# Output projection of two heads with three products: the high parts stacked by transfers, the low halves summed on VectorE

## The chip, the cores and the metric

One core of a Trainium2 chip runs the whole program. Its engines (TensorE or PE with its weight loads PEld, VectorE or DVE, ScalarE or ACT, GpSimd or POOL, and the queue SP that issues transfers) run at the same time, each through its own program in order; they meet only at semaphores. The metric is the device time of one launch in microseconds (us); lower is better.

## The reference

Four blocks on x of 4 x 512 x 256 in fp32: attention with low-rank keys and values, a gated feed-forward net, a state-space scan, the feed-forward net again. The change is in the attention's last step.

```python
kv_up = (kv_c @ wkv_up.T).reshape(bs, seq_len, NH, D_NOPE + D_V)   # kv_c: 64 numbers a token
v = kv_up[..., D_NOPE:]
scores = jnp.where(causal, einsum('bqhd,bkhd->bhqk', q, k) * scale, -inf)
probs = softmax(scores)
out = einsum('bhqk,bkhd->bqhd', probs, v).reshape(bs, seq_len, NH * D_V)
return out @ wo.T                                                  # 16 heads -> 256
```

## The kernel before

**Precision by pairs.** TensorE multiplies in a reduced type (fp32r), so each factor is kept as a high part (rounded by ScalarE) and a low part (VectorE subtracts the high part from the exact value), and a product is three matmuls: high·high, high·low, low·high.

**The value side.** The 64 numbers `kv_c` of a token stand for keys and values of all heads. `v_hl` holds their high part in columns 0 to 63 and their low part in 64 to 127, and the per-head map from 64 numbers to the 256 outputs (`wo_a`, `wo_b`) is made once in eight preparation tasks `t_vo` (lines 381 to 400), two heads each. So `values` leaves in `bank[6]`, for four heads of 128 queries (512 columns), the product with the values' high half in partitions 0 to 63 and the one with their low half in 64 to 127. The attention output is the sum of the two.

**The output projection.** `wo_a` holds the high part of the map in both halves of the partitions, `wo_b` its low part in 0 to 63 and its high part in 64 to 127. `out_high` (ScalarE, L881 and L883) copies all 128 partitions of bank 6 to `o_a` and partitions 0 to 63 once more to `o_b`; `out_low` (VectorE, L1211) puts the remainder of partitions 0 to 63 into partitions 64 to 127 of `o_b`. `project` (TensorE) then makes two products of 128 x 256 for each head, `o_a`·`wo_a` (L1600) and `o_b`·`wo_b` (L1602), eight for a unit.

**Units and slots.** A unit is four heads of one tile of 128 queries; a batch has 16 units (`n`), the program 64. With tile i (0 to 3) a unit has i + 1 blocks of keys. Every engine runs slots `s`: TensorE, ScalarE and VectorE each do in slot s a fixed list of steps of several units at once, written out by hand in `pe_slot`, `act_slot` and `dve_slot`. Unit n has its scores in slots n+2 and n+3, its values in slot n+5 and its projection near the end of slot n+6 of TensorE. VectorE ends its slot n+4 with `out_low(n)`; behind it stand, in the next slot, `recip` (L1188), `pt_low` (L1205) and `row_max` (L1153). TensorE waits for `out_low(n)` at the first `values` matmul of unit n+1, since bank 6 exists once; behind that wait stand transposes (L1573) and scores (L649 to L651) that ScalarE and VectorE work on next. `exp` is L846, `normalise` L866, `pt_high` L875.

**The rest.** SP issues the loads at the start, then waits and loads `ssm_nat` for the third block, then stores the output. GpSimd looks up the feed-forward weights until about 540 us.

Of the kernel before, what the change touches and what calls it, by code (L numbers as in the profile page):

```python
# [4 lines left out]
F32 = mybir.dt.float32  # L5
F32R = mybir.dt.float32r
BF16 = mybir.dt.bfloat16
I32 = mybir.dt.int32
ALU = mybir.AluOpType
ACT = mybir.ActivationFunctionType  # L10

P = 128
# [95 lines left out]
def build(nc, x_in, wq_down, wq_up, wq_rope, q_norm_w, wkv_down, kv_norm_w, wkv_up, wk_rope, wo,  # L108
# [3 lines left out]
    with ctx:  # L112
# [58 lines left out]
        wo_b = r1("wo_b", [P, HEADS, DIM], F32R)  # L171
# [31 lines left out]
        o_b = r2("o_b", [P, 2, G, P], F32R)  # L203
# [29 lines left out]
        def sem(name):  # L233
            return ctx.enter_context(nc.semaphore(name))
# [29 lines left out]
        o_hi_s, o_lo_s, y_mm = sem("o_hi_s"), sem("o_lo_s"), sem("y_mm")  # L264
        x_add, f_add, s_add = sem("x_add"), sem("f_add"), sem("s_add")
# [117 lines left out]
        def t_vo(k):  # L383
# [8 lines left out]
            def act(e, o):  # L392
                nc.scalar.copy(wo_a[:, 2 * k:2 * k + 2, :], o[:, :].rearrange("p (h n) -> p h n", h=2))
                return nc.scalar.copy(wo_b[KR:P, 2 * k:2 * k + 2, :], o[KR:P, :].rearrange("p (h n) -> p h n", h=2))

            def dve(e, o):
                return nc.vector.tensor_tensor(wo_b[0:KR, 2 * k:2 * k + 2, :],
                                               o[0:KR, :].rearrange("p (h n) -> p h n", h=2),
                                               wo_a[0:KR, 2 * k:2 * k + 2, :], ALU.subtract)
# [301 lines left out]
        def _(sp_):  # L701
# [30 lines left out]
            sp_.wait_ge(tok, token_count(BATCH, 0))  # L732
            sp_.wait_ge(at_mm, 1 + 3 * BATCH)
            sp_.dma_start(ssm_nat[:, 0, :, :], w_in.rearrange("(c p) d -> p c d", p=P)).then_inc(ssm_in, 16)
            sp_.dma_start(ssm_nat[:, 2, :, :], w_out.rearrange("(c p) d -> p c d", p=P)).then_inc(ssm_in, 16)
            hpc = P // (DIM // 32)
            for c in range(CK):
                sp_.dma_start(ssm_nat[:, 1, c, :],
                              w_dt[c * hpc:(c + 1) * hpc, :].unsqueeze(1).to_broadcast([hpc, DIM // 32, DIM]))\
                    .then_inc(ssm_in, 16)  # L740
# [52 lines left out]
        def _(act):  # L793
# [84 lines left out]
            def out_high(b, n):  # L878
                act.wait_ge(pv_mm, b * BLOCKS + blocks_before(n + 1))
                free_after(act, y_mm, b * UNITS + n - 1)  # L880
                nc.scalar.copy(o_a[:, n % 2, :, :].rearrange("p h d -> p (h d)"), bank[6][:, :])\  # L881
                    .then_inc(o_hi_s, 1)
                nc.scalar.copy(o_b[0:KR, n % 2, :, :].rearrange("p h d -> p (h d)"), bank[6][0:KR, :])\  # L883
                    .then_inc(o_hi_s, 1)
# [204 lines left out]
        def _(dve):  # L1089
# [119 lines left out]
            def out_low(b, n):  # L1209
                dve.wait_ge(o_hi_s, 2 * (b * UNITS + n) + 2)  # L1210
                nc.vector.tensor_tensor(o_b[KR:P, n % 2, :, :].rearrange("p h d -> p (h d)"), bank[6][0:KR, :],  # L1211
                                        o_a[0:KR, n % 2, :, :].rearrange("p h d -> p (h d)"), ALU.subtract)\
                    .then_inc(o_lo_s, 1)
# [289 lines left out]
        def _(pe):  # L1503
# [89 lines left out]
            def project(b, n):  # L1593
                g = n % (HEADS // G)
                pe.wait_ge(o_hi_s, 2 * (b * UNITS + n) + 2)
# [3 lines left out]
                for h in range(G):  # L1599
                    nc.tensor.matmul(bank[7][:, 0:DIM], o_a[:, n % 2, h, :], wo_a[:, g * G + h, :],  # L1600
                                     start=g == 0 and h == 0, stop=False)
                    last = nc.tensor.matmul(bank[7][:, 0:DIM], o_b[:, n % 2, h, :], wo_b[:, g * G + h, :],  # L1602
                                            start=False, stop=g == HEADS // G - 1 and h == G - 1)
# [253 lines left out]
```

## Time and profile before

| | us |
|---|---|
| median of 3 runs | 822.56 (821.38 to 823.37) |
| the profiled execution | 816.43, of it 814.6 in the span |
| first projection to last (L1600) | 85.7 to 561.2 |
| busy in the span: PE, DVE, ACT | 752.5, 675.2, 607.2 |

Busy time of an engine is the time in which at least one of its instructions runs. Durations of neighbours on one engine overlap in the records, so what an instruction costs a full engine is the distance from its start to the next one's start, not its duration. A wait is given as "engine, what it ran next, <- who ended the wait"; "issue" means that the profile shows no one who did.

### The profile page before, as it was taken

Reading aid. Unit: us, or ns where it says so; the run is one execution under the profiler, and the core shown is the slowest. Engines: PE = TensorE matmul, PEld = TensorE weight load, DVE = VectorE, ACT = ScalarE, POOL = GpSimd, SP = SyncE. Lnnn points to the kernel's source line nnn. Section 1 sums busy time; section 2 is a strip of 40 time slices with the busy share of each in tenths; the row PEclk is TensorE's granted clock in tenths of the full one; section 3 lists DMA queues with packets and bytes.
Section 4 is the critical chain, followed back from the end, with each engine's and each line's share of the span. In section 5 each row is a group of like instructions: output and inputs, shape, how many; then the busy total and the mean of one; then the engine's idle time right before and its main releaser. Section 6 shows DMA issues by size and latency. Waiting matters only on the chain.

```text
span 814.6 us, 15156 instructions
## 1 busy us (share of the span) xinstructions
PE 752.5 (92%) x4556; PEld 648.2 (80%) x4556; DVE 675.2 (83%) x2208; ACT 607.2 (75%) x1508; POOL 462.1 (57%) x388
## 2 busy tenths in 40 slices
PE   4788999999999999999998999999998999999998
PEld 4667888888878788888887888777887788897887
DVE  4986899998899998899998899997775878777643
ACT  2457999987999887999987899895436566674222
POOL 0379999999999999999999999910000000000000
PEclk9988999999999999999999999999999999999999
DMA  9710000000000000000000100000000000000000
GB/s 233 241 53 1 2 1 2 1 1 1 1 2 1 1 2 2 1 2 1 2 1 1 40 2 1 1 1 1 1 1 0 1 1 1 1 1 27 27 27 27
DMA packets 15377, 14.54 MB, mean 18 GB/s; under 512 B 5792, under 2 KB 14432, under 8 KB 15040
## 3 DMA queue, kind: packets, MB, share of 16 engines
q1 hardware_dynamic: 13792, 11.41, 4.8%
q0 software_dynamic: 624, 2.12, 0.8%
q8 instruction: 38, 0.62, 0.3%
q14 instruction: 43, 0.35, 0.1%
q10 hardware_dynamic: 880, 0.04, 0.1%
HBM read 11.46 MB, written 2.10 MB: 17 GB/s over the span
## 4 chain that ended last, share of the span: by engine, by line
PE 57%; DVE 16%; ACT 15%; issue 11%; DMA 1%; DVEq 0%; ACTq 0%; SPq 0%
PE bank L649 11%; PE bank L651 11%; PE bank L650 11%; PE bank L1573 6%; ACT prob L866 5%; ACT prob L846 3%; PE bank L1587 2%; PE bank L1590 2%; DVE pt_lo L1205 2%; ACT pt_hi L875 2%; PE bank L1600 2%; PE bank L1602 2%; PE bank L614 1%; DVE o_b L1211 1%; DVE bias_m L1153 1%
## 5 line engine op out<-in xcount | busy, mean ns | idle before, releaser
L782 POOL TENSOR_SCALAR hot<-raw_gu,lut 128x352 f32<-128x352 int32 x120 | 178.1, 1484 | 12.2
L788 POOL TENSOR_TENSOR total<-total,hot 128x352 f32<-128x352 f32 (+1 forms) x168 | 159.4, 949 | 14.0
L846 ACT ACTIVATE prob<-bank,bias_m 128x128 f32<-128x128 f32 (+3 forms) x256 | 136.2, 532 | 19.4 <-DVE bias_m L1153 19.0
L1153 DVE CUSTOM_DVE_ANT_0 bank<-bank,mask 128x128 f32<-128x128 f32 (+3 forms) x256 | 125.8, 495 | 23.5 <-issue 21.9
L866 ACT ACTIVATE prob<-prob,rden 128x128 f32<-128x128 f32 (+3 forms) x224 | 110.6, 545 | 8.2 <-DVE rden L1188 7.3
L1205 DVE TENSOR_TENSOR pt_lo<-bank,pt_hi 128x512 fp32r<-128x512 f32 x160 | 109.1, 682 | 8.7 <-ACT pt_hi L875 8.3
L1573 PE MATMUL bank<-ident,prob 128*128 128x128 f32 x640 | 99.8, 279 | 15.0 <-ACT prob L866 9.1
L875 ACT CAST pt_hi<-bank 128x512 fp32r<-128x512 f32 x160 | 94.1, 589 | 13.0 <-PE bank L1590 7.2
L1573 PEld LDWEIGHTS bank<-ident,prob 128*128 128x128 f32 x640 | 73.3, 141 | 33.4 <-ACT prob L866 18.6
L649 PE MATMUL bank<-kt_hi,qt_hi 128*128 128x128 f32 (+3 forms) x256 | 87.6, 342 | 3.2 <-ACT prob L846 2.5
L782 POOL TENSOR_SCALAR hot<-raw_dn,lut 128x352 f32<-128x352 int32 (+1 forms) x60 | 87.0, 1451 | 6.1
L651 PE MATMUL bank<-kt_hi,qt_lo 128*128 128x128 f32 (+3 forms) x256 | 83.2, 325 | 0.0
L650 PE MATMUL bank<-kt_lo,qt_hi 128*128 128x128 f32 (+3 forms) x256 | 83.2, 325 | 0.0
L1587 PE MATMUL bank<-pt_hi,v_hl 128*128 128x512 f32 x160 | 68.5, 428 | 3.7 <-issue 3.5
L649 PE MATMUL bank<-xt_hi,gu_hi 128*128 128x512 f32 (+1 forms) x176 | 70.2, 399 | 1.7 <-DVE h_f L1345 1.6
L651 PE MATMUL bank<-xt_hi,gu_lo 128*128 128x512 f32 (+1 forms) x176 | 69.5, 395 | 0.0
L650 PE MATMUL bank<-xt_lo,gu_hi 128*128 128x512 f32 (+1 forms) x176 | 69.4, 394 | 0.0
L1600 PE MATMUL bank<-wo_a,o_a 128*128 128x256 f32 x256 | 67.9, 298 | 0.1
L957 ACT ACTIVATE silu<-bank 128x512 f32<-128x512 f32 x40 | 24.0, 600 | 57.5 <-PE bank L651 57.5
L1590 PE MATMUL bank<-pt_lo,v_hl 128*128 128x512 f32 x160 | 63.6, 398 | 0.3 <-DVE pt_lo L1205 0.2
L1602 PE MATMUL bank<-wo_b,o_b 128*128 128x256 f32 x256 | 63.7, 282 | 0.0
L649 PEld LDWEIGHTS bank<-kt_hi,qt_hi 128*128 128x128 f32 x256 | 49.2, 192 | 13.1 <-ACT prob L846 3.6
(215 smaller groups left out, 2092.7 us busy)
## 6 DMA issues: line engine op xcount, KB each, us to landing
x<-in_L_attn_a_x_dram SPq DMA_DIRECT2D x4, 512.0 KB, 8.1
wo_nat<-in_L_attn_a_wo_dram SPq DMA_DIRECT2D x1, 2048.0 KB, 15.5
out_dram<-x SPq DMA_DIRECT2D x16, 128.0 KB, 1.8
wqu<-in_L_attn_a_wq_up_dram SPq DMA_DIRECT2D x2, 768.0 KB, 8.3
wqr<-in_L_attn_a_wq_rope_dram SPq DMA_DIRECT2D x4, 192.0 KB, 7.0
raw_dn<-in_L_ffn_down_idx_dram POOLq DMA_DIRECT2D x1, 688.0 KB, 6.7
raw_gu<-in_L_ffn_gate_idx_dram POOLq DMA_DIRECT2D x1, 640.0 KB, 5.2
raw_gu<-in_L_ffn_up_idx_dram POOLq DMA_DIRECT2D x1, 640.0 KB, 5.7
```

What stands on the lines that cost most here:

```text
L649: nc.tensor.matmul(o, l_hi, r_hi, start=start and k == 0, stop=False)
L650: nc.tensor.matmul(o, l_hi, r_lo, start=False, stop=False)
L651: last = nc.tensor.matmul(o, l_lo, r_hi, start=False, stop=stop and k == n - 1)
L782: nc.gpsimd.tensor_scalar((hot if v else total)[:, 0:n], raw[:, c:c + n], float(v), lut[:, v:v + 1], ALU.is_equal, ALU.mult).then_inc(lut_ ...
L788: nc.gpsimd.tensor_tensor(dst, total[:, 0:n], hot[:, 0:n], ALU.add).then_inc(lut_sum, 1)
L846: nc.scalar.activation(prob[:, n % 2, h, 0:w], bank[2 + h % 2][:, 0:w], ACT.Exp, bias=bias_m[:, n % 2, h:h + 1], scale=-1.0, accum_out=den ...
L866: nc.scalar.activation(prob[:, n % 2, h, 0:w], prob[:, n % 2, h, 0:w], ACT.Copy, scale=rden[:, n % 2, h:h + 1]).then_inc(norm_a, 1)
L875: nc.scalar.copy(pt_hi[:, c % 2, :, :].rearrange("p h d -> p (h d)"), bank[4 + c % 2][:, :])\
L1153: nc.vector.tensor_tensor_reduce(out=bank[2 + h % 2][:, 0:w], in0=bank[2 + h % 2][:, 0:w], in1=mask[:, TB * P - w:TB * P], scale=1.0, scal ...
L1205: nc.vector.tensor_tensor(pt_lo[:, c % 2, :, :].rearrange("p h d -> p (h d)"), bank[4 + c % 2][:, :], pt_hi[:, c % 2, :, :].rearrange("p h ...
L1573: last = nc.tensor.transpose(bank[4 + c % 2][:, h * P:(h + 1) * P], prob[:, n % 2, h, j * P:(j + 1) * P], ident[:, :])
L1587: nc.tensor.matmul(bank[6][:, :], v, pt_hi[:, c % 2, :, :].rearrange("p h d -> p (h d)"), start=j == 0, stop=False)
```

## The change

For two heads there are three products instead of four. VectorE adds the product with the values' low half (partitions 64 to 127 of bank 6) to the remainder, so `o_a` now holds the high part of partitions 0 to 63 above and "remainder plus low half" below, and is multiplied with `wo_a` for each head. `o_b` holds only high parts: that of an even head in partitions 0 to 63, that of the odd head beside it in 64 to 127, multiplied with a `wo_b` that has the map's low parts of the two heads stacked in the same way. Two transfers between SBUF and SBUF for each unit, issued by SP, copy the high parts into `o_b`. The loads of `ssm_nat` come behind the transfers of the first unit of the last batch.

```diff
-        wo_b = r1("wo_b", [P, HEADS, DIM], F32R)
+        wo_b = r1("wo_b", [P, HEADS // 2, DIM], F32R)
...
-        o_b = r2("o_b", [P, 2, G, P], F32R)
+        o_b = r2("o_b", [P, 2, G // 2, P], F32R)
+        o_rest = r2("o_rest", [P, G, P], F32)
...
             def act(e, o):
-                nc.scalar.copy(wo_a[:, 2 * k:2 * k + 2, :], o[:, :].rearrange("p (h n) -> p h n", h=2))
-                return nc.scalar.copy(wo_b[KR:P, 2 * k:2 * k + 2, :], o[KR:P, :].rearrange("p (h n) -> p h n", h=2))
+                return nc.scalar.copy(wo_a[:, 2 * k:2 * k + 2, :], o[:, :].rearrange("p (h n) -> p h n", h=2))
 
             def dve(e, o):
-                return nc.vector.tensor_tensor(wo_b[0:KR, 2 * k:2 * k + 2, :],
-                                               o[0:KR, :].rearrange("p (h n) -> p h n", h=2),
-                                               wo_a[0:KR, 2 * k:2 * k + 2, :], ALU.subtract)
+                for j, rows in enumerate((slice(0, KR), slice(KR, P))):
+                    last = nc.vector.tensor_tensor(wo_b[rows, k, :], o[rows, j * DIM:(j + 1) * DIM],
+                                                   wo_a[rows, 2 * k + j, :], ALU.subtract)
+                return last
...
+            def duplicate(b, n):
+
+                sp_.wait_ge(o_hi_s, b * UNITS + n + 1)
+                for j, rows in enumerate((slice(0, KR), slice(KR, P))):
+                    sp_.dma_start(o_b[rows, n % 2, :, :].bitcast(F32), o_a[0:KR, n % 2, j::2, :].bitcast(F32))\
+                        .then_inc(o_dup[n % 2], 16)
+
+            for b in range(BATCH):
+                for n in range(UNITS):
+                    duplicate(b, n)
+                    if b == BATCH - 1 and n == 0:
+                        load_ssm()
...
             def out_high(b, n):
                 act.wait_ge(pv_mm, b * BLOCKS + blocks_before(n + 1))
                 free_after(act, y_mm, b * UNITS + n - 1)
-                nc.scalar.copy(o_a[:, n % 2, :, :].rearrange("p h d -> p (h d)"), bank[6][:, :])\
-                    .then_inc(o_hi_s, 1)
-                nc.scalar.copy(o_b[0:KR, n % 2, :, :].rearrange("p h d -> p (h d)"), bank[6][0:KR, :])\
+                nc.scalar.copy(o_a[0:KR, n % 2, :, :].rearrange("p h d -> p (h d)"), bank[6][0:KR, :])\
                     .then_inc(o_hi_s, 1)
...
             def out_low(b, n):
-                dve.wait_ge(o_hi_s, 2 * (b * UNITS + n) + 2)
-                nc.vector.tensor_tensor(o_b[KR:P, n % 2, :, :].rearrange("p h d -> p (h d)"), bank[6][0:KR, :],
-                                        o_a[0:KR, n % 2, :, :].rearrange("p h d -> p (h d)"), ALU.subtract)\
-                    .then_inc(o_lo_s, 1)
+                dve.wait_ge(o_hi_s, b * UNITS + n + 1)
+                rest = o_rest[KR:P, :, :].rearrange("p h d -> p (h d)")
+                nc.vector.tensor_tensor(rest, bank[6][0:KR, :], o_a[0:KR, n % 2, :, :].rearrange("p h d -> p (h d)"),
+                                        ALU.subtract).then_inc(o_rest_s, 1)
+                dve.wait_ge(o_rest_s, b * UNITS + n + 1)
+                nc.vector.tensor_tensor(o_a[KR:P, n % 2, :, :].rearrange("p h d -> p (h d)"), rest, bank[6][KR:P, :],
+                                        ALU.add).then_inc(o_lo_s, 1)
...
-                pe.wait_ge(o_hi_s, 2 * (b * UNITS + n) + 2)
+                pe.wait_ge(o_hi_s, b * UNITS + n + 1)
+                pe.wait_ge(o_dup[n % 2], 32 * ((b * UNITS + n) // 2 + 1))
                 pe.wait_ge(o_lo_s, 1 + b * UNITS + n + 1)
...
-                for h in range(G):
-                    nc.tensor.matmul(bank[7][:, 0:DIM], o_a[:, n % 2, h, :], wo_a[:, g * G + h, :],
-                                     start=g == 0 and h == 0, stop=False)
-                    last = nc.tensor.matmul(bank[7][:, 0:DIM], o_b[:, n % 2, h, :], wo_b[:, g * G + h, :],
-                                            start=False, stop=g == HEADS // G - 1 and h == G - 1)
+                for j in range(G // 2):
+                    for h in (2 * j, 2 * j + 1):
+                        nc.tensor.matmul(bank[7][:, 0:DIM], o_a[:, n % 2, h, :], wo_a[:, g * G + h, :],
+                                         start=g == 0 and h == 0, stop=False)
+                    last = nc.tensor.matmul(bank[7][:, 0:DIM], o_b[:, n % 2, j, :], wo_b[:, g * G // 2 + j, :],
+                                            start=False, stop=g == HEADS // G - 1 and j == G // 2 - 1)
```

How it stands on VectorE, where one slot ends with `out_low` and the next begins (a unit of tile 2; the names in brackets are the semaphores that an instruction waits for). Before:

```order
L1153 ISA bias_m 128x1
L1211 TENSOR_TENSOR o_b<-bank,o_a 64x512 [waits o_hi_s]
L1188 RECIPROCAL rden<-den 128x2 [waits norm_a,s_exp]
L1205 TENSOR_TENSOR pt_lo<-bank,pt_hi 128x512 [waits pv_mm,pt_hi_s]
L1188 RECIPROCAL rden<-den 128x2 [waits norm_a,s_exp]
```

and now (the lines' numbers have moved: L1188 is L1203, L1205 is L1220):

```order
L1168 ISA bias_m 128x1
L1227 TENSOR_TENSOR o_rest<-bank,o_a 64x512 [waits o_hi_s]
L1230 TENSOR_TENSOR o_a<-o_rest,bank 64x512 [waits o_rest]
L1203 RECIPROCAL rden<-den 128x2 [waits norm_a,s_exp]
L1220 TENSOR_TENSOR pt_lo<-bank,pt_hi 128x512 [waits pv_mm,pt_hi_s]
L1203 RECIPROCAL rden<-den 128x2 [waits norm_a,s_exp]
```

An instruction over 512 columns, with a wait for the one ahead of it, has come between `out_low` and everything behind it.

On TensorE, the projection of such a unit before:

```order
L1600 MATMUL bank<-wo_a,o_a 128x256 [waits o_lo_s,o_hi_s]
L1602 MATMUL bank<-wo_b,o_b 128x256
L1600 MATMUL bank<-wo_a,o_a 128x256
L1602 MATMUL bank<-wo_b,o_b 128x256
L1600 MATMUL bank<-wo_a,o_a 128x256
L1602 MATMUL bank<-wo_b,o_b 128x256
L1600 MATMUL bank<-wo_a,o_a 128x256
L1602 MATMUL bank<-wo_b,o_b 128x256
L1573 MATMUL bank<-ident,prob 128x128 [waits pt_lo_s]
```

and now:

```order
L1620 MATMUL bank<-wo_a,o_a 128x256 [waits o_lo_s,o_dup1,o_hi_s]
L1620 MATMUL bank<-wo_a,o_a 128x256
L1622 MATMUL bank<-wo_b,o_b 128x256
L1620 MATMUL bank<-wo_a,o_a 128x256 x2
L1622 MATMUL bank<-wo_b,o_b 128x256
L1591 MATMUL bank<-ident,prob 128x128 [waits pt_lo_s]
```

Two of eight matmuls are gone, and the first waits for the transfers as well.

On ScalarE, `out_high` of such a unit before:

```order
L875 CAST pt_hi<-bank 128x512 [waits pv_mm,pt_mm]
L881 CAST o_a<-bank 128x512 [waits y_mm,pv_mm]
L883 CAST o_b<-bank 64x512
L846 ACTIVATE prob,den<-bank,bias_m 128x384 [waits s_max]
```

and now:

```order
L892 CAST pt_hi<-bank 128x512 [waits pv_mm,pt_mm]
L898 CAST o_a<-bank 64x512 [waits y_mm,pv_mm]
L863 ACTIVATE prob,den<-bank,bias_m 128x384 [waits s_max]
```

The second copy has gone from each unit.

## Rows read from the trace of the kernel before

**Rows 1.** The profile's page: busy time by engine, and the closing chain by engine.
```profile
PE 752.5 (92%) x4556; PEld 648.2 (80%) x4556; DVE 675.2 (83%) x2208; ACT 607.2 (75%) x1508; POOL 462.1 (57%) x388
...
PE 57%; DVE 16%; ACT 15%; issue 11%; DMA 1%; DVEq 0%; ACTq 0%; SPq 0%
```

**Rows 2.** Busy time by stretch: all projections; tile 0 and tile 2 of batch 2.
```profile
core 0: us, PE busy (x) PEld busy (x) DVE busy (x) ACT busy (x) POOL busy (x), PEclk, DMA share, GB/s
...
86.00:562.00 476.00, 451.88 (x2828) 388.34 (x2826) 437.93 (x1515) 433.75 (x1174) 415.48 (x341) 1.00 0.01 3
...
329.00:354.60 25.60, 24.78 (x170) 22.07 (x169) 21.91 (x93) 25.47 (x91) 23.84 (x20) 1.00 0.00 1
...
384.60:419.90 35.30, 34.43 (x206) 29.07 (x205) 33.13 (x101) 32.11 (x76) 32.80 (x28) 1.00 0.00 1
```

**Rows 3.** VectorE's waits from 86 to 562 us: total, times, longest.
```profile
DVE bank L1153 <- issue: 17.2, 40, 1.1
DVE pt_lo L1205 <- ACT pt_hi L875: 8.3, 14, 1.3
DVE o_b L1211 <- ACT o_b L883: 2.0, 2, 1.7
```

**Rows 4.** Instructions that touch `o_b`: count, shortest/median/longest in ns.
```profile
L1211 DVE TENSOR_TENSOR o_b<-bank,o_a x64: 683/684/689, 79.8 to 559.3; 64x512 fp32r<-64x512 f32 x64
```

**Rows 5.** VectorE in order of time, the end of a slot: start, duration, instruction.
```profile
475.16 0.68 DVE L1205 TENSOR_TENSOR pt_lo<-bank,pt_hi 128x512 fp32r<-128x512 f32 x1
475.77 0.42 DVE L1153 CUSTOM_DVE_ANT_0 bank<-bank,mask 128x256 f32<-128x256 f32 x1
...
476.12 0.14 DVE L1153 DVE_READ_ACCUMULATOR2_ANT bias_m<- 128x1 f32 x1
476.29 0.68 DVE L1211 TENSOR_TENSOR o_b<-bank,o_a 64x512 fp32r<-64x512 f32 x1
477.00 0.17 DVE L1188 RECIPROCAL rden<-den 128x2 f32<-128x2 f32 x1
477.08 0.67 DVE L1205 TENSOR_TENSOR pt_lo<-bank,pt_hi 128x512 fp32r<-128x512 f32 x1
```

**Rows 6.** ScalarE in order of time, the second copy and what follows.
```profile
481.39 0.59 ACT L883 CAST o_b<-bank 64x512 fp32r<-64x512 f32 x1
481.87 0.48 ACT L846 ACTIVATE prob<-bank,bias_m 128x256 f32<-128x256 f32 x1
```

**Rows 7.** TensorE in order of time, inside a projection.
```profile
482.63 0.28 PE L1600 MATMUL bank<-wo_a,o_a 128*128 128x256 f32 x1
482.75 0.28 PE L1602 MATMUL bank<-wo_b,o_b 128*128 128x256 f32 x1
```

**Rows 8.** Preparation of `wo_b`, second four tasks: ScalarE, VectorE, then TensorE's wait.
```profile
61.94 0.58 ACT L394 CAST wo_b<-bank 64x512 fp32r<-64x512 f32 x1
...
66.16 0.68 DVE L397 TENSOR_TENSOR wo_b<-bank,wo_a 64x512 fp32r<-64x512 f32 x1 [0.52 <-ACT wo_b L394]
...
66.89 0.64 PEld L614 LDWEIGHTS bank<-ident,xn 128*128 128x128 f32 x6 [3.38 <-DVE wo_b L397]
```

**Rows 9.** Transfers by line: queue, count, KB each, median us from issue to landing.
```profile
ssm_nat<-in_L_attn_b_W_in_dram SPq DMA_DIRECT2D x1, 256.0 KB, 3.2
...
ident<-in_ident_dram SPq DMA_DIRECT2D x1, 64.0 KB, 1.9
```

**Rows 10.** From a unit's high copy to its projection: a tile-0 unit, then the last.
```profile
451.21 0.59 ACT L881 CAST o_a<-bank 128x512 fp32r<-128x512 f32 x1
...
457.74 0.33 PE L1600 MATMUL bank<-wo_a,o_a 128*128 128x256 f32 x1
...
558.25 0.58 ACT L881 CAST o_a<-bank 128x512 fp32r<-128x512 f32 x1 [1.32 <-PE bank L1590]
...
560.17 0.36 PE L1600 MATMUL bank<-wo_a,o_a 128*128 128x256 f32 x1
```

**Rows 11.** Busy time by stretch, columns as in rows 2: the start of the last batch.
```profile
445.00:450.00 5.00, 3.24 (x16) 2.93 (x15) 3.80 (x15) 2.09 (x9) 4.63 (x5) 0.72 0.36 99
```

More of the change, by code:

```diff
@@ L264, in build @@
         o_hi_s, o_lo_s, y_mm = sem("o_hi_s"), sem("o_lo_s"), sem("y_mm")
+        o_rest_s = sem("o_rest")
+        o_dup = [sem(f"o_dup{k}") for k in range(2)]
         x_add, f_add, s_add = sem("x_add"), sem("f_add"), sem("s_add")
@@ L729, in _, with load_ssm @@
             sp_.dma_start(wv2[:, :, 0, :], kvu[1]).then_inc(wv_in, 16)
[L732 to L740, printed above, removed]
+            def load_ssm():
+                sp_.wait_ge(tok, token_count(BATCH, 0))
+                sp_.wait_ge(at_mm, 1 + 3 * BATCH)
+                sp_.dma_start(ssm_nat[:, 0, :, :], w_in.rearrange("(c p) d -> p c d", p=P)).then_inc(ssm_in, 16)
+                sp_.dma_start(ssm_nat[:, 2, :, :], w_out.rearrange("(c p) d -> p c d", p=P)).then_inc(ssm_in, 16)
+                hpc = P // (DIM // 32)
+                for c in range(CK):
+                    sp_.dma_start(ssm_nat[:, 1, c, :],
+                                  w_dt[c * hpc:(c + 1) * hpc, :].unsqueeze(1).to_broadcast([hpc, DIM // 32, DIM]))\
+                        .then_inc(ssm_in, 16)
+            def duplicate(b, n):
[8 more added lines that the diff above has]
+                        load_ssm()
             for b in range(BATCH):
```

## The prediction, made before the changed kernel had run

> **What bounds the kernel now.** I read the page first [rows 1]: TensorE is busy for 92% of the span, and 57% of the closing chain lies on it. Taken alone that says that every matmul removed is a gain. But it is an average over the program, and the change acts only while projections run, so I read the busy time of that stretch next [rows 2]. From 86 to 562 us, 476 us long, TensorE is busy for 451.9 us (95%), VectorE for 437.9 (92%), ScalarE for 433.8 (91%). Three engines are nearly full at once. VectorE has 38.1 us in which nothing of it runs, and no more. The two shorter stretches show how the lead changes: in tile 0 of batch 2 ScalarE is full (25.5 of 25.6 us) and VectorE has room (21.9), in tile 2 TensorE is full (34.4 of 35.3) and VectorE is close behind (33.1). The third view is what VectorE's idle time is [rows 3]: 17.2 us in 40 waits ahead of the row maximum (no releaser is shown; by the program it is the scores of TensorE), 8.3 us in 14 waits for ScalarE's `pt_hi`, 2.0 us for ScalarE's second copy; waits under a microsecond nearly all. With some smaller ones these are about 30 us; the other 8 us are gaps of 0.03 us between instructions and won't go.
>
> So the question is what the change does to VectorE, not to TensorE.
>
> **TensorE.** Two of the eight projection matmuls of a unit go. Inside a projection a matmul starts 0.12 us after the one ahead of it (482.63 to 482.75, [rows 7]); its 0.28 us duration is mostly overlap. 64 units x 2 x 0.12 = 15.4 us less work, 436.5 us of 476. That is a gain only where TensorE is what the others wait for.
>
> **ScalarE.** The second copy goes; the next instruction started 0.48 us after it (481.39 to 481.87, [rows 6]). 64 x 0.48 = 30.7 us less, 403 us of 476. The first copy now covers 64 partitions instead of 128, which I cost at nothing: the two copies, of 128 and of 64 partitions, have the same 0.6 us within 0.02 [rows 6, 10].
>
> **VectorE.** It gets one more instruction of 64 partitions x 512 for each unit, 64 in all. There is no such add in the trace; two rows bound it. `pt_low`, also 512 columns from PSUM and SBUF, takes 0.61 us from its start to the next start (475.16 to 475.77, [rows 5]); the present `out_low` takes 0.71 (476.29 to 477.00), as it starts only when the instruction ahead has ended and the one behind starts only when it has ended itself [rows 5]; all 64 have that duration [rows 4]. The add waits for its neighbour ahead and writes to partitions 64 to 127 as `out_low` does, so I take 0.71: 64 x 0.71 = 45.4 us (39.0 at the lower end). VectorE then has 437.9 + 45.4 = 483.3 us of work plus 8 us of gaps for a stretch that lasts 476. It becomes the bound, whatever TensorE saves. Queued behind the add on VectorE are the reciprocal, `pt_low` and the next row maximum; those who wait for them are ScalarE's normalisation and exponentials, and TensorE at the first `values` matmul of the next unit, which now waits for the add.
>
> **How much idle time takes up the add.** This is the unsure term. ScalarE's work ahead of `pt_hi` is 0.48 us shorter in each unit while VectorE comes 0.71 later, so the 8.3 + 2.0 us of waits for ScalarE should vanish. Of the 17.2 us ahead of the row maximum I let 7 go: the waits that stand behind `out_low` -> `values` -> scores -> row maximum move along with `out_low` and stay, since that path gets longer itself. So 17 of 30 us are taken up; the ends are 0 and 30.
>
> **The end of attention.** For the last unit there is no slot between copy and projection. Its copy starts at 558.25 and lasts 0.58; its projection starts at 560.17, 1.34 us behind the copy's end [rows 10]. The transfers begin at the copy's end; no transfer from SBUF to SBUF is in the trace. The nearest rows are one of 64 KB that landed in 1.9 us and one of 256 KB in 3.2 [rows 9]; at 1.9 to 3.2, and up to 0.5 more for the second of the pair, TensorE stands 0.6 to 2.4 us longer. I take 1.5.
>
> **The other 63 units.** A tile-0 unit, the shortest, has its copy end at 451.80 and its projection at 457.74 [rows 10]: 5.9 us for a landing of 1.9 to 3.7 us. I cost these transfers at nothing; the slot between is their cover. If it were gone, each unit would pay what the landing exceeds 5.9 us by. SP has nothing else to do then, and the moved loads of `ssm_nat` are needed only behind attention: nothing.
>
> **Preparation.** In the second four tasks that make `wo_b`, ScalarE's second copies set the pace (0.6 us each) and VectorE waits 0.52 us ahead of a subtraction; TensorE waits until the last one, 3.38 us in all [rows 8]. Four copies fewer are 2.4 us, and the subtraction in two halves gives back about 1 us; the first four tasks lie in VectorE's own order and lose about as much as they win. I take -1.0 (between -3 and +1.5).
>
> **The sum**, against the profiled execution of 816.4 us: + 45.4 (add) - 17 (idle time taken up) + 1.5 (last unit) - 1.0 (preparation) = + 28.9, so 845.3 us. The median of the runs is 822.56, 6.1 us above the profiled execution, and the same + 28.9 gives 851.5.
>
> A rule of the Trainium skill bears on the rows of `out_low`. The row shows that it neither overlaps the instruction ahead nor the one behind [rows 5]. "VectorE: DVE Perf Modes", section "Two Vector instructions with no wait between them", has a model for that: a Vector instruction whose input or output begins in another group of 32 partitions than the last one in the same memory is held until all earlier ones have finished. Here the trace agrees for `out_low` (from partition 0 to 64), and by the rule the add is held too, and it counts as well that it reads PSUM from partition 64: the next PSUM read from partition 0, behind the reciprocal, is held in turn.
>
> **Rivals.**
> 1. *The add costs more than itself.* Now the instruction behind the reciprocal starts 0.08 us after it, inside its 0.17 us (477.00 to 477.08, [rows 5]). If it has to wait for its end and the usual 0.03 us, that is 0.12 us more in each unit, 7.7 us: 816.4 + 28.9 + 7.7 = 853.0, median 859.2. For it: `out_low` shows this behaviour. Against: no row here shows a PSUM read being held two instructions later. This is what the rule above would give. Chance 0.17.
> 2. *The idle time goes entirely.* With a lighter TensorE and ScalarE VectorE never waits, and the add overlaps like `pt_low`: 39.0 - 30 + 1.5 - 1.0 = + 9.5, median 832 (838.5 with the add at 0.71). For it: in tile 0 VectorE's load with the add, 21.9 + 4 x 0.71 = 24.7 us of 25.6, would still fit [rows 2]. Against: in tile 2 it wouldn't (33.1 + 2.8 of 35.3, with the gaps), and each engine runs in its own order, so that all three have idle time today beside one another. Chance 0.15.
> 3. *Faster: TensorE is the bound and the add is hidden.* Then TensorE's 15.4 us come off: 822.56 - 15.4 - 1.0 = 806. The chain's 57% on TensorE speaks for it [rows 1]. It decides if VectorE's free time exceeds the add's, 38.1 us against at least 39.0 [rows 2], so it needs the add below 0.6 us, cheaper than any 512-column instruction there. Chance 0.03.
> 4. *The transfers are late.* With a landing of 7 us instead of under 4, the tile-0 units and then most others would wait 1.1 us in front of the projection, and all behind it: up to 64 x 1.1 = 70 us, median 921. Against it stands [rows 9]. Chance 0.02.
> 5. *TensorE's clock.* At the start of the last batch TensorE is busy for only 3.24 of 5 us, behind a long step of VectorE (`split_values`), and the granted clock of these 5 us is 0.72, a mixture of full (2.4 GHz) and half speed (1.2) [rows 11]: 2.8 us at half speed, 1.4 us of work lost. A VectorE that leads by more could do that in more places: at 1.4 us each and some 7 places about + 10 on top, median 861. Chance 0.05.
> That the change doesn't do what it says is excluded by the order of the instructions: copies, matmuls and transfers stand there as described.
>
> **The numbers.** Forecast 0.58; its own range, from the idle time taken up (10 to 27 of 30) and the add at 0.71, is + 19 to + 37, so 842 to 859. Rivals 0.17, 0.15, 0.03, 0.02, 0.05. The range for 8 in 10 goes down into rival 2 and up through rivals 1 and 5: 836 to 870. A difference of 0.2% is about what a measurement of this kernel can tell from none. Faster by more 0.03, within it 0.02, slower 0.95.
>
> **What would show it.** Right: from first to last projection some 505 us instead of 476, VectorE busy for 97% of it, TensorE near 86% and ScalarE near 80%, and the chain mostly on VectorE; the add 0.71 us from start to start; waits for `pt_hi` gone; transfers landing in under 4 us and no wait of TensorE on them but the last. Wrong: waits of TensorE for transfers; a VectorE still 5% idle; matmuls of the projection 0.24 us apart.

## The result and the profile after

| | before | changed |
|---|---|---|
| median of the runs, us | 821.97 (4) | 860.28 (4) |
| lowest, highest | 818.63, 823.37 | 859.71, 860.92 |
| the profiled execution (span) | 816.43 (814.6) | 859.80 (857.9) |
| first to last projection | 475.5 | 515.6 |

The changed kernel takes 1.048 times as long, 95% interval 1.0435 to 1.0519: 38.3 us more by the medians, 43.4 us between the two profiled executions, of which that of before is one of the fastest of its kernel (its executions here lie between 812.5 and 825.3 us), so differences of a few us are taken from medians, and traces serve to show where time lies.

The page of the changed kernel, its busy times and its closing chain (they answer to [rows 1]):

```profile
PE 758.4 (88%) x4428; PEld 635.4 (74%) x4428; DVE 728.6 (85%) x2280; ACT 581.6 (68%) x1436; POOL 461.2 (54%) x388
...
PE 35%; DVE 33%; issue 24%; ACT 6%; DVEq 1%; DMA 1%; SPq 0%; ACTq 0%
```

TensorE has 128 matmuls fewer and its share of the chain has fallen from 57% to 35%; VectorE has 53 us more work and twice its share. The same by stretch, columns as in [rows 2]: ahead of the first projection, from the first to the end of the last, behind it.

```profile
0.00:87.28 87.28, 62.58 (x340) 55.10 (x341) 65.52 (x230) 40.60 (x123) 48.70 (x49) 0.90 0.44 125
87.28:602.90 515.62, 453.85 (x2694) 371.60 (x2693) 487.42 (x1577) 413.28 (x1109) 412.48 (x340) 1.00 0.09 19
602.90:857.90 255.00, 241.99 (x1400) 208.75 (x1398) 175.69 (x474) 127.71 (x205) 0.00 (x0) 0.99 0.03 9
```

Before, the three were 85.7, 475.5 and 253.4 us long. So 40.1 of the 43.4 us lie where the change acts. There VectorE is now busy for 487.4 of 515.6 us (before: 437.6 of 475.5), 49.9 us more, and idle for 28.2 us instead of 37.9. 49.9 - 9.7 is the 40 us: VectorE's new work shows in full except for 10 us of its idle time. VectorE's waits in that stretch (they answer to [rows 3]):

```profile
DVE bank L1168 <- issue: 6.4, 15, 1.2
DVE pt_lo L1220 <- ACT pt_hi L892: 6.1, 13, 1.2
DVE o_rest L1227 <- ACT o_a L898: 1.2, 1, 1.2
DVE qt_lo L1192 <- ACT qt_hi L875: 0.8, 2, 0.4
```

They were about 30 us and are 14.5; the other idle time, gaps of some 0.03 us between instructions, grew from 8.1 to 13.7 us. The others now wait for VectorE; ScalarE's waits, and TensorE's at the next unit's first `values` matmul:

```profile
ACT prob L883 <- DVE rden L1203: 41.6, 67, 2.2
ACT prob L863 <- DVE bias_m L1168: 33.0, 52, 1.6
...
PE bank L1605 <- DVE o_a L1230: 14.8, 26, 1.1
```

Where the add stands, in order of time on VectorE (it answers to [rows 5]):

```profile
511.36 0.13 DVE L1168 DVE_READ_ACCUMULATOR2_ANT bias_m<- 128x1 f32 x1
511.53 0.69 DVE L1227 TENSOR_TENSOR o_rest<-bank,o_a 64x512 f32<-64x512 f32 x1
512.25 0.69 DVE L1230 TENSOR_TENSOR o_a<-o_rest,bank 64x512 fp32r<-64x512 f32 x1
512.97 0.17 DVE L1203 RECIPROCAL rden<-den 128x2 f32<-128x2 f32 x1
513.17 0.69 DVE L1220 TENSOR_TENSOR pt_lo<-bank,pt_hi 128x512 fp32r<-128x512 f32 x1
```

The add takes 0.72 us from start to start, and `pt_low` starts 0.20 us after the reciprocal, where it was 0.08 [rows 5]. Before, `out_low` to `pt_low` was 0.79 us; now it is 1.64. `pt_low` stands directly behind the reciprocal in 35 of the 64 units, and there it is 0.08 us in all of them before and 0.20 in all of them now; in most of the others VectorE does a step of another kind in between. Over all units, the first read of PSUM behind `out_low` overlapped the instruction ahead of it 50 times before and never does now.

The transfers, all 128 of them (time on SP's queue in ns, and landing):

```profile
L750 SPq DMA_DIRECT2D o_b<-o_a x128: 590/604/1164, 80.1 to 599.9; - x128
...
DMA to landing us min/median/max: 2.0/2.1/4.2
```

Only the last unit's made TensorE wait (L1620 <- DMA, 1.9 us, once):

```profile
598.70 0.59 ACT L898 CAST o_a<-bank 64x512 fp32r<-64x512 f32 x1 [1.32 <-PE bank L1608]
...
602.10 0.47 PE L1620 MATMUL bank<-wo_a,o_a 128*128 128x256 f32 x2 [1.85 <-DMA o_b<-o_a]
```

### The profile page after: what moved, and what is told of

Its sections match the earlier page's. It is cut to its first block, busy times and chain, and to the rows that moved or that the text cites. A ratio compares the mean times of both kernels' runs of the same rounds, so it can differ in the third digit from the quotient of the medians.

```text
span 857.9 us, 15044 instructions
## 1 busy us (share of the span) xinstructions
PE 758.4 (88%) x4428; PEld 635.4 (74%) x4428; DVE 728.6 (85%) x2280; ACT 581.6 (68%) x1436; POOL 461.2 (54%) x388
## 4 chain that ended last, share of the span: by engine, by line
PE 35%; DVE 33%; issue 24%; ACT 6%; DVEq 1%; DMA 1%; SPq 0%; ACTq 0%
PE bank L652 9%; PE bank L654 8%; PE bank L653 8%; DVE pt_lo L1220 7%; DVE o_rest L1227 5%; DVE bias_m L1168 3%; ACT prob L883 2%; DVE qt_lo L1192 2%; DVE q_tok L1182 2%; DVE rden L1203 1%; PE bank L1591 1%; PE bank L617 1%; DVE bank L1168 1%; ACT prob L863 1%; DVE q_rot L1185 1%
## 5 line engine op out<-in xcount | busy, mean ns | idle before, releaser
L1220 DVE TENSOR_TENSOR pt_lo<-bank,pt_hi 128x512 fp32r<-128x512 f32 x160 | 109.9, 687 | 8.2 <-ACT pt_hi L892 6.1
L1591 PEld LDWEIGHTS bank<-ident,prob 128*128 128x128 f32 x640 | 72.2, 141 | 53.0 <-ACT prob L883 25.5
L892 ACT CAST pt_hi<-bank 128x512 fp32r<-128x512 f32 x160 | 93.3, 583 | 16.8 <-PE bank L1591 8.7
L1605 PE MATMUL bank<-pt_hi,v_hl 128*128 128x512 f32 x160 | 72.3, 452 | 20.5 <-DVE o_a L1230 15.4
L652 PE MATMUL bank<-kt_hi,qt_hi 128*128 128x128 f32 (+3 forms) x256 | 87.3, 341 | 1.6 <-ACT prob L863 1.3
L1605 PEld LDWEIGHTS bank<-pt_hi,v_hl 128*128 128x128 f32 x160 | 30.1, 188 | 36.3 <-DVE o_a L1230 28.1
L1620 PE MATMUL bank<-wo_a,o_a 128*128 128x256 f32 x256 | 52.6, 297 | 1.9 <-DMA o_b<-o_a 1.9
```

The source lines that it names most:

```text
L652: nc.tensor.matmul(o, l_hi, r_hi, start=start and k == 0, stop=False)
L892: nc.scalar.copy(pt_hi[:, c % 2, :, :].rearrange("p h d -> p (h d)"), bank[4 + c % 2][:, :])\
L1220: nc.vector.tensor_tensor(pt_lo[:, c % 2, :, :].rearrange("p h d -> p (h d)"), bank[4 + c % 2][:, :], pt_hi[:, c % 2, :, :].rearrange("p h ...
L1591: last = nc.tensor.transpose(bank[4 + c % 2][:, h * P:(h + 1) * P], prob[:, n % 2, h, j * P:(j + 1) * P], ident[:, :])
L1605: nc.tensor.matmul(bank[6][:, :], v, pt_hi[:, c % 2, :, :].rearrange("p h d -> p (h d)"), start=j == 0, stop=False)
```

## The theories

**A.** VectorE's load is the bound now, and the add is the cost: what VectorE has to do more in a unit, whoever waits for it, shows in the time; the savings of TensorE and ScalarE are worth little. **B.** The transfers cost a good part. **C.** It is not the load but the path: the add lies between one unit's values and the next unit's, which share bank 6. **D.** (for VectorE's price per unit) the first partition of an instruction's operands decides if it overlaps its neighbours.

To see where the time goes, the distances between VectorE's successive `out_low` instructions were added up by the tile of the unit that ends them (16 units a tile, the first unit has none; us, from the starts in each trace):

| kernel | tile 0 | tile 1 | tile 2 | tile 3 |
|---|---|---|---|---|
| before | 95.9 | 115.8 | 139.4 | 128.4 |
| changed | 101.0 | 128.5 | 146.2 | 142.9 |
| e1_no_add | 93.4 | 113.7 | 137.0 | 128.6 |
| e4_add_elsewhere | 101.5 | 126.8 | 145.0 | 135.4 |
| e6_before_add | 99.7 | 130.8 | 144.9 | 143.0 |
| e7_after_norm_act | 100.3 | 126.4 | 144.1 | 145.9 |
| e5_before_transfer | 94.6 | 115.4 | 139.1 | 127.5 |
| e8_before_transfer_norm_act | 93.3 | 114.2 | 136.5 | 137.2 |

## The add: taken out, moved, and put alone into the kernel before

**Taken out** of the changed kernel:

```diff
-                nc.vector.tensor_tensor(rest, bank[6][0:KR, :], o_a[0:KR, n % 2, ...], ALU.subtract).then_inc(o_rest_s, 1)
-                dve.wait_ge(o_rest_s, b * UNITS + n + 1)
-                nc.vector.tensor_tensor(o_a[KR:P, n % 2, ...], rest, bank[6][KR:P, :], ALU.add).then_inc(o_lo_s, 1)
+                nc.vector.tensor_tensor(o_a[KR:P, n % 2, ...], bank[6][0:KR, :], o_a[0:KR, n % 2, ...],
+                                        ALU.subtract).then_inc(o_lo_s, 1)
```

> The changed kernel without the add: out_low writes its remainder straight to the lower half of o_a, so the product with the values' low half is left out of the output. Theory A (VectorE's load is the bound, and the add is the cost): VectorE is back at its load of before, TensorE and ScalarE stay lighter by 15 and 31 us, so 806 to 820 us, under the kernel before. Theory B (the transfers between SBUF and SBUF cost a good part of the 38 us): 835 or more. Theory C (not VectorE's load but the longer way from the values over the add to the next values matmul): 806 to 820 as well.

Measured: 813.6 us, 0.9924 of the kernel before (0.9896 to 0.9951). The transfers, the six matmuls and the single copy are all still there, and the time is 47 us under the changed kernel and 8 under the kernel before. B is out: 835 or more was expected of it. A and C both hold. (By the two profiled executions, 817.6 and 816.4 us, there would be no gain over the kernel before; the 8 us are those of the medians.)

**Moved**: as e1, with an addition of the same size for which nobody waits.

```diff
+            def filler(b, n):
+                nc.vector.tensor_tensor(o_rest[0:KR, :, :]..., mask[0:KR, :], mask[0:KR, :], ALU.add)
...
                 do(row_max, s - 2, 1)
+                do(filler, s - 4)
```

> As e1_no_add, but VectorE gets an addition of 64 partitions x 512 columns in each unit at another place of the slot (behind the second row maximum), from a constant into o_rest, for which nobody waits; the values' low half is left out of the output as there. Theory A: 64 x 0.6 us of VectorE's time come back, less what idle time takes up: e1 plus 25 to 38 us, 835 to 855. Theory C: hidden, e1 plus under 6 us. Theory B says nothing here.

Measured: 850.0 us, 1.0352 (1.0303 to 1.0401), 36.4 us more than e1 for 64 instructions, 0.57 us each. C is out as the main cause: off the path the instruction costs nearly its own time. What the add costs beyond that in its real place (860.3 - 850.0 = 10 us) is not taken apart by a run. By the table 7.5 of it lie in tile 3. Three things differ: the read of PSUM behind the reciprocal, held in the changed kernel alone (64 x 0.12 = 7.7 us at most); VectorE's normalisations in tile 3, which last 22.6 us in the changed kernel and 18.0 here; and TensorE's wait for the add at the next `values` matmul, 14.8 us against 1.2 here, which is the path of C. So C may have a part in these 10 us. The filler's durations, whose median is above the add's 691 ns:

```profile
L1231 DVE TENSOR_TENSOR o_rest<-mask x64: 673/734/1432, 77.7 to 587.6; 64x512 f32<-64x512 f32 x64
```

**Alone in the kernel before**, with its eight matmuls and both copies:

```diff
-                nc.vector.tensor_tensor(o_b[KR:P, n % 2, ...], bank[6][0:KR, :], o_a[0:KR, n % 2, ...], ALU.subtract)\
-                    .then_inc(o_lo_s, 1)
+                low = o_b[KR:P, n % 2, :, :].rearrange("p h d -> p (h d)")
+                nc.vector.tensor_tensor(low, bank[6][0:KR, :], o_a[0:KR, n % 2, ...], ALU.subtract).then_inc(o_rest_s, 1)
+                dve.wait_ge(o_rest_s, b * UNITS + n + 1)
+                nc.vector.tensor_tensor(low, low, bank[6][KR:P, :], ALU.add).then_inc(o_lo_s, 1)
```

> The kernel before with one part of the change alone: behind out_low an add of bank 6's lower half onto the remainder (64 x 512, with its wait), so the output counts that half twice. Eight matmuls a unit and ScalarE's second copy stay. Theory A: VectorE's load is that of the changed kernel and the two other savings are worth little beside it: 860 to 872. If the savings of TensorE and ScalarE were all worth their 15 and 31 us: 880 or more.

Measured: 859.1 us, 1.0469 (1.0418 to 1.0520): the changed kernel's time, a little below the range that was expected. Busy from the first to the last projection, columns as in [rows 2]:

```profile
88.60:603.00 514.40, 462.24 (x2820) 386.62 (x2819) 486.35 (x1577) 439.55 (x1173) 411.61 (x339) 1.00 0.01 3
```

VectorE's 486 us are those of the changed kernel (487), ScalarE has 26 us more than there and TensorE its 128 matmuls back. Neither shows by more than these measurements tell: 1.2 us by the medians, in favour of e6, and 0.2 us by the table. With the add in place, the rest of the three-product scheme gains nothing measurable.

## The transfers: replaced, and alone

**Replaced** by two copies of 64 x 256 on ScalarE in the changed kernel:

```diff
+                for j, rows in enumerate((slice(0, KR), slice(KR, P))):
+                    nc.scalar.copy(o_b[rows, n % 2, :, :], heads(bank[6])[0:KR, j::2, :]).then_inc(o_hi_s, 1)
...
-                pe.wait_ge(o_dup[n % 2], 32 * ((b * UNITS + n) // 2 + 1))
```

> The changed kernel with its two transfers in each unit replaced by two copies of 64 x 256 on ScalarE, straight from PSUM; everything else as changed. Theory A and C: ScalarE has room and the last unit no longer waits for a transfer, so 856 to 862. Theory B: 845 or less.

Measured: 859.2 us, 1.0472 (1.0408 to 1.0536), 1.1 us under the changed kernel. That is what A expected, and well above the 845 of B. The difference itself is within the spread (857.1 to 861.7); in the traces the last unit's projection starts 2.25 us after its high copy's end instead of 2.81. `out_low` now waits for all three copies, which costs VectorE little: 2.3 us of waits for ScalarE there in all, against 1.2.

**Alone** in the kernel before, in place of ScalarE's second copy:

```diff
-                nc.scalar.copy(o_b[0:KR, n % 2, ...], bank[6][0:KR, :]).then_inc(o_hi_s, 1)
...
+                    sp_.wait_ge(o_hi_s, b * UNITS + n + 1)
+                    sp_.dma_start(o_b[0:KR, n % 2, :, :].bitcast(F32), o_a[0:KR, n % 2, :, :].bitcast(F32))\
+                        .then_inc(o_dup[n % 2], 16)
...
-                dve.wait_ge(o_hi_s, 2 * (b * UNITS + n) + 2)
+                dve.wait_ge(o_hi_s, b * UNITS + n + 1)
```

> The kernel before with one part of the change alone: the second copy of ScalarE replaced by one transfer between SBUF and SBUF of the same 64 x 512, with its wait in front of the projection. Nothing is added to VectorE, nothing taken from TensorE. Theory A: ScalarE 31 us lighter where it and the two others are all nearly full, so 814 to 821. If the transfers cost: 822 to 835.

Measured: 814.7 us, 0.9928 (0.9898 to 0.9958) over 12 runs. This part of the change is a gain of 0.7%, and the kernel beats both. Where it lies the traces don't show: the two profiled executions (816.2 and 816.4 us) are alike, and the table gives 2.9 us of the 7. The edit also lets `out_low` start behind ScalarE's first copy instead of its second; VectorE's waits there are 1.2 us in all, and were 2.0, so the lighter ScalarE is the likelier reason, but no run separates the two. Its distance to e1, which has TensorE's saving as well, is 1.1 us by the medians, less than the intervals of the two (some 2 us each way), and 3.9 us by the table: at the load of before, 15 us of TensorE's work are worth 1 to 4 us, though TensorE is busy for 95% of the stretch [rows 2].

## What an instruction costs VectorE: the first partition

**The remainder in partitions 0 to 63** of `o_rest` in the changed kernel:

```diff
-                rest = o_rest[KR:P, :, :].rearrange("p h d -> p (h d)")
+                rest = o_rest[0:KR, :, :].rearrange("p h d -> p (h d)")
```

> The changed kernel with the remainder kept in partitions 0 to 63 of o_rest instead of 64 to 127, so that the subtraction reads and writes from partition 0 like the instruction ahead of it. If what holds an instruction back is the change of its first partition, the subtraction overlaps its neighbour ahead again (about 0.1 us a unit, 6 us in all) while the add and what follows it stay held: 852 to 857. If it is held for another reason (its wait for ScalarE): 858 to 861. The trace tells by the distance from the row maximum's end to the subtraction's start.

Measured: 847.4 us (four executions from 843.8 to 852.3), 1.033 (1.0259 to 1.0401): 13 us less than the changed kernel, twice what was expected. In order of time on VectorE:

```profile
499.86 0.43 DVE L1168 CUSTOM_DVE_ANT_0 bank<-bank,mask 128x256 f32<-128x256 f32 x1
...
500.20 0.14 DVE L1168 DVE_READ_ACCUMULATOR2_ANT bias_m<- 128x1 f32 x1
500.20 0.68 DVE L1227 TENSOR_TENSOR o_rest<-bank,o_a 64x512 f32<-64x512 f32 x1
500.92 0.69 DVE L1230 TENSOR_TENSOR o_a<-o_rest,bank 64x512 fp32r<-64x512 f32 x1
501.64 0.17 DVE L1203 RECIPROCAL rden<-den 128x2 f32<-128x2 f32 x1
501.84 0.69 DVE L1220 TENSOR_TENSOR pt_lo<-bank,pt_hi 128x512 fp32r<-128x512 f32 x1
```

The subtraction now starts together with the read of the accumulator, not 0.17 us after its start as in the changed kernel (511.36 to 511.53) and before (476.12 to 476.29, [rows 5]). That is so in all 62 units in which such a read stands ahead of it: 0.00 us here, 0.16 to 0.17 in both others. It has the same wait for ScalarE, so D holds for it. 64 x 0.17 = 10.9 us fit what the traces show: from the first to the last projection the profiled execution is 10.1 us shorter than the changed kernel's; another 2.7 us lie ahead of the first projection, where nothing was changed. I had expected 0.1, the distance lost behind `out_low`; the loss ahead of it is larger. The reciprocal behind the add and the `pt_low` behind the reciprocal stay held (0.72 and 0.20). The model that the prediction took from the Trainium skill ("VectorE: DVE Perf Modes", section "Two Vector instructions with no wait between them") says just this: by it the subtraction is held no more, while the reciprocal and the `pt_low` still are. The trace agrees in these three places. The add's own start says nothing on it, as it also waits for the subtraction by semaphore.

**The same swap in the kernel before**: the remainder to partitions 0 to 63 of `o_b`, the high part to 64 to 127, and `wo_b` likewise.

```diff
-                nc.scalar.copy(o_b[0:KR, n % 2, ...], bank[6][0:KR, :])
+                nc.scalar.copy(o_b[KR:P, n % 2, ...], bank[6][0:KR, :])
...
-                nc.vector.tensor_tensor(o_b[KR:P, n % 2, ...], bank[6][0:KR, :], ...
+                nc.vector.tensor_tensor(o_b[0:KR, n % 2, ...], bank[6][0:KR, :], ...
```

> The kernel before with the two halves of o_b (and of wo_b) swapped: the remainder goes to partitions 0 to 63, where the subtraction reads it, and ScalarE copies the high part to 64 to 127. The same instructions, only the first partitions differ. If the change of first partition costs VectorE what e3_rest_low suggests (0.17 us ahead of out_low, and 0.1 behind it), VectorE is 11 to 17 us lighter; with TensorE and ScalarE as full as before a third to a half of that shows: 813 to 819. If first partitions don't matter: 820 to 823.

Measured: 818.6 us, 0.9983 (0.9950 to 1.0015). That is at the edge of the 813 to 819 that were expected if first partitions count, but a difference from the kernel before can't be told. And with the high part brought there by a transfer:

```diff
-                    sp_.dma_start(o_b[0:KR, n % 2, :, :].bitcast(F32), o_a[0:KR, n % 2, :, :].bitcast(F32))\
+                    sp_.dma_start(o_b[KR:P, n % 2, :, :].bitcast(F32), o_a[0:KR, n % 2, :, :].bitcast(F32))\
```

> e11_swap with the high part brought to partitions 64 to 127 by one transfer between SBUF and SBUF in place of ScalarE's second copy (as in e5_before_transfer). VectorE 11 to 17 us lighter, ScalarE 31 us, TensorE as before and then the bound: 802 to 811. If it gives no more than e5_before_transfer (TensorE's order is all that is left): 813 to 816.

Measured: 813.7 us, 0.9910 (0.9873 to 0.9947), the lowest of those kernels that compute the whole output, but within 1 us of e5_before_transfer. So the second of the two expectations came true, not the 802 to 811. The instructions do overlap:

```profile
481.16 0.14 DVE L1161 DVE_READ_ACCUMULATOR2_ANT bias_m<- 128x1 f32 x1
481.16 0.68 DVE L1219 TENSOR_TENSOR o_b<-bank,o_a 64x512 fp32r<-64x512 f32 x1
481.76 0.14 DVE L1196 RECIPROCAL rden<-den 128x2 f32<-128x2 f32 x1
481.87 0.69 DVE L1213 TENSOR_TENSOR pt_lo<-bank,pt_hi 128x512 fp32r<-128x512 f32 x1
```

From the accumulator's read to `pt_low` it is 0.71 us, where before it was 0.96 (476.12 to 477.08). That is up to 16 us of VectorE's time, and 1 us of the kernel's, within the noise. At the load of before VectorE is not the bound; 0.84 us more in each unit makes it one. A saving of 0.17 us a unit is worth 10 to 13 us in the changed kernel, and one of up to 0.25 us a unit nothing measurable in the kernel before.

## Work moved from VectorE to ScalarE

```diff
 def on_dve(n, h):
-    return tile_of(n % UNITS) == TB - 1 and h >= 2
+    return False
```

> The changed kernel with the 32 normalisations of tile 3 that VectorE does (484 to 776 ns each) given to ScalarE. Theory A: VectorE loses 32 x 0.45 to 0.7 us, 14 to 22, ScalarE has 100 us of room: 838 to 848. If ScalarE's order in the slots of tile 3 gets in the way: 850 to 860.

Measured: 856.8 us, 1.0433 (1.0377 to 1.0489), 3.5 us less than the changed kernel, not the 12 to 22 that A alone expected. VectorE's busy time in the stretch falls from 487.4 to 468.7 us and ScalarE has room, but the units of tile 3, where the work was moved, take 145.9 us instead of 142.9 (table above). This is the second of the two cases that were written down (850 to 860). What VectorE gained, the path gave back there: TensorE's transposes of a unit wait for all four normalised heads, and by the program ScalarE does the third and fourth only at the start of its next slot. ScalarE's `pt_hi` needs these transposes, and VectorE's `pt_low` needs `pt_hi`. The waits of TensorE's weight loads for the normalised heads, and of VectorE for `pt_hi`, over the whole execution:

```profile
PEld bank L1591 <- ACT prob L883: 36.7, 58, 1.7
...
DVE pt_lo L1220 <- ACT pt_hi L892: 24.3, 36, 1.1
```

In the changed kernel they are 25.5 and 6.1 us. Of VectorE's 24.3 us, 22.0 lie in the units of tile 3: VectorE does 18.7 us less work and waits 18.2 us longer.

The same edit in e5_before_transfer:

> As e5_before_transfer, and the 32 normalisations of tile 3 that VectorE does given to ScalarE, whose load then is 15 us under that of before while VectorE's is 15 to 20 under it and TensorE alone is full: 803 to 815. If ScalarE's order in tile 3 gets in the way: 816 to 825.

Measured: 822.5 us, 1.0015 (0.9987 to 1.0044), 7.8 us slower than e5_before_transfer, with 137.2 us in tile 3 against 127.5. VectorE's waits for `pt_hi` are 26.6 us there against 8.0. Freed ScalarE time didn't buy this; its order got in the way, again the second of the two cases that were written down.

## Why the prediction was right, and where it was not

The time (860.3) lies in the range of 836 to 870, and the direction and mechanism are those of the forecast; the forecast (851.5) was 9 us short, and the time lies just above the 842 to 859 that it allowed itself. The range holds it because it was widened upwards for rivals 1 and 5. From the first to the last projection the forecast had 29.9 us (45.4 - 17 + 1.5), and 40.1 were measured. The terms that missed, below, are the held reads of PSUM (some 6 us), the normalisations (4.5) and the idle time taken up (15.3 instead of 17); together they come to 12 us for the 10 that are missing.

- **VectorE becomes the bound**: right, shown by e1, e4 and e6. It followed from one row, 437.9 of 476 us busy, with an add that had to be above 0.6 us. The argument that 0.6 us would be "cheaper than any 512-column instruction there" was wrong: the normalisations over 128 x 512, which touch no PSUM, have a median of 484 ns (below). That VectorE's load is the bound does not make every saving on it count: e7 took 18.7 us off it and won 3.5.
- **The add, 64 x 0.71 = 45.4**: right, 0.72 measured, in all 64. Its duration is 691 ns, its part of the busy time 44 us.
- **Behind the reciprocal**: the mechanism of the first rival, which had been given a chance of 0.17, came true, 0.20 instead of 0.08 us. Its 64 x 0.12 = 7.7 us count every unit; only 50 of them had an overlap to lose, so it is nearer to 6 us. With the full term the forecast would have been 859.2; that this comes so near to 860.3 is partly luck, as the normalisations were missing from it. It had been left out of the sum as no row showed a PSUM read held two instructions later; the rule that gave it was the better guide.
- **Idle time taken up, 17 us**: about right in size as far as waits go (from 29.8 to 14.5 us), wrong in its parts. The gaps that "won't go" grew by 5.6 us, so VectorE's idle time as a whole fell by only 9.7. The waits for ScalarE were to vanish and fell only from 10 to 8; those ahead of the row maximum were to keep 10 and kept 6. By tile the rise is 5.1, 12.7, 6.8 and 14.5 us for some 13 us of new work each: tiles 0 and 2 had room, tiles 1 and 3 none. I had looked at tiles 0 and 2 only, and had read tile 2 as having hardly any; it took up half.
- **Not in the sum**: VectorE's 32 normalisations in place. They have 22.6 us of busy time after and 18.1 before, + 4.5. In pairs they take 0.88 us in the last batch once GpSimd has finished, and up to 1.9 while it runs. But GpSimd at work does not always stretch them: of the 13 pairs beside it in the kernel before, 6 took 0.88 or 0.89, and of the 12 in the changed kernel none (1.10 at least). That GpSimd is what stretches them, and why the changed kernel meets it worse, wasn't tried by itself.

```profile
L1211 DVE TENSOR_SCALAR prob<-prob,rden x32: 476/776/1220, 163.5 to 589.4; 128x512 f32<-128x512 f32 x32
```

```profile
L1196 DVE TENSOR_SCALAR prob<-prob,rden x32: 476/484/1253, 156.8 to 549.0; 128x512 f32<-128x512 f32 x32
```

The first line is the changed kernel's, the second that of before.

- **The last unit, 1.5 us**: right. From its copy's end to its projection it is now 2.8 us (599.29 to 602.10), before 1.34. About half of that would be there without a transfer: in e6, with the add and no transfer, it is 2.06. What followed was not foreseen: TensorE's granted clock was 0.81 and 0.85 in the next two stretches of 5 us, against 1.00 before. Between full (2.4 GHz) and half speed (1.2 GHz) these are 1.9 and 1.5 us at half, so 1.7 us of work lost, which fits the 1.6 us that everything behind attention takes longer.

```profile
600.00:605.00 5.00, 3.15 (x19) 2.84 (x18) 3.04 (x5) 1.90 (x4) 0.00 (x0) 0.81 0.15 30
605.00:610.00 5.00, 5.00 (x19) 3.95 (x19) 4.50 (x17) 2.53 (x5) 0.00 (x0) 0.85 0.00 2
```

  TensorE had stood still for 1.85 us ahead of it, but this is not shown to be the reason. The same wait for the last transfer, 1.84 or 1.85 us, stands in five profiled executions, and the clock fell behind it in three (the changed kernel, e1 and e3) and not in two (e4 and e7). In e6 and e10 it fell elsewhere behind attention. These five with a lower clock take 254.6 to 254.9 us behind the last projection, all the others 253.2 to 253.6. The same place in e4:

```profile
592.90:597.90 5.00, 5.00 (x29) 4.39 (x30) 3.10 (x8) 3.05 (x5) 0.00 (x0) 1.00 0.01 3
```

- **Preparation, -1.0**: the first projection starts at 87.3 us instead of 85.7, but in e1, e3, e4, e7 and e2, with the same preparation, it starts at 90.1, 84.6, 87.5, 85.4 and 86.0 us. The term is below what one execution tells.
- **The other transfers at nothing**: right, 2.1 us to landing and no wait but the last. **TensorE's 15.4 us and ScalarE's 30.7 at nothing**: right beside the add (e6). In the kernel before the two together are worth 8 us (e1), the copy most of it (e5, 7 us).
- **The signs written down**: the add at 0.71 us from start to start, transfers landing in under 4 us (2.1 in the median, 4.2 at most) and ScalarE near 80% (80.2) came. Not so: 515.6 us instead of 505; TensorE 88% instead of 86; VectorE 94.5% instead of 97; a chain mostly on VectorE (33%, TensorE 35%); waits for `pt_hi` gone (6.1 us left). VectorE is idle for 5.5% of the stretch, and "a VectorE still 5% idle" had been put down as a sign of being wrong. It was a poor sign: 13.7 of the 28.2 us are the gaps between instructions, and e4, where more work on VectorE alone cost 36 us, shows 25 us idle as well. But it says that the three engines still wait for one another, and VectorE's load alone is not the whole account.

## What to carry to other kernels

When three engines are each over 90% busy, ask of every instruction that is moved who has less idle time than it costs; that engine sets the result, and savings on the others are worth little. A saving on that engine counts only if the work's new place delays nobody (e7: 18.7 us of load taken off, 3.5 us won). Count an instruction by its distance from start to start with its real neighbours: operands that begin at another partition cost 0.17 us ahead and 0.1 behind here. A copy that only duplicates data can go to a transfer if a slot lies between (814.7 us, 0.9928), and this part of the change is the one to keep.

## What was not expected of the hardware

The loss ahead of an instruction whose first partition changes (0.17 us, since it waits for the accumulator's read and 0.03 us more) was larger than the loss behind it (0.1 us). A pair of in-place normalisations on VectorE took 0.88 us with GpSimd at rest and between 0.88 and 1.9 with GpSimd at work. And after the same wait of 1.85 us TensorE's granted clock fell in three executions (to 0.66 to 0.70 in the 5 us behind the last projection) and stayed at 1.00 in two.
